# Delta-rule recurrence: bias carried by a weight row, v projected after the middle, late decays on VectorE, GpSimd's list reordered

## What is computed

```python
q = silu(causal_conv4(x @ Wq.T) + qcb)      # k (times 1/8) and v likewise, with kcb and vcb
a, beta = sigmoid(x @ Wa.T + ba), sigmoid(x @ Wb.T + bb)
def step(S, t):                              # S: 64 x 64 for each batch and head
    err = S @ k[t] - v[t]
    S = a[t][:, None] * S - beta[t] * err[:, None] * k[t][None, :]
    return S, S @ q[t]
o = layernorm(o, 64) * ln_w + ln_b           # then * sigmoid(x @ Wg.T), @ Wo.T, and x + that
```

## Time and profile before

| | |
|---|---|
| median of 3 runs | 4325.35 us (4315.23 to 4333.77) |
| the profiled execution | 4334.36 us, its span 4332.6 us |
| mean granted TensorE clock | 0.868 of full |
| TensorE, VectorE, ScalarE, GpSimd busy | 82%, 67%, 48%, 54% of the span |
| instructions | 127508 |

### The profile page before, as it was taken

How to read it: one execution, slowest core, us unless ns; L and a number is a source line. 1 busy time by engine, 2 the same in 40 slices (tenths; PEclk the granted TensorE clock), 3 DMA queues, 4 the chain that set the end, 5 groups by cost and what they waited for, 6 DMA issues and landing times. The chain is left out here.

```text
span 4332.6 us, 127508 instructions
## 1 busy us (share of the span) xinstructions
PE 3540.3 (82%) x53697; PEld 2464.3 (57%) x53697; DVE 2885.8 (67%) x6344; ACT 2090.6 (48%) x4778; POOL 2320.5 (54%) x3045
## 2 busy tenths in 40 slices
PE   6777888788787888878778777466999989988998
PEld 4555565555565556555555545354566647765765
DVE  4666666766667666666666766423788878865885
ACT  4243334343344333333333433233788869945992
POOL 1656566665666666676566666443101028815870
PEclk9788788887888888888788988668999989998999
DMA  3101110110111111011010101140000001101110
GB/s 83 33 27 36 29 35 26 39 35 25 36 29 35 33 32 35 25 39 36 24 34 26 34 28 30 34 131 28 2 2 2 2 21 37 41 15 30 38 41 25
DMA packets 156313, 140.11 MB, mean 32 GB/s; under 512 B 65350, under 2 KB 108578, under 8 KB 155486
## 3 DMA queue, kind: packets, MB, share of 16 engines
q1 hardware_dynamic: 153438, 129.25, 10.9%
q0 software_dynamic: 2304, 2.71, 0.2%
HBM read 96.12 MB, written 16.82 MB: 26 GB/s over the span
## 5 line engine op out<-in xcount | busy, mean ns | idle before, releaser
L1227 DVE TENSOR_TENSOR a_tmp<-a_h,banks 128x128 f32<-128x128 f32 (+6 forms) x896 | 434.1, 484 | 271.1 <-POOL a_h L944 252.2
L1233 DVE TENSOR_REDUCE a_h<-a_tmp 128x64 f32<-128x128 f32 (+6 forms) x896 | 434.2, 485 | 17.5
L1253 DVE STREAM_TRANSPOSE a_cross<-banks 128x1024 f32<-128x1024 f32 x64 | 80.0, 1250 | 449.6 <-PE banks L649 449.6
L944 POOL TENSOR_TENSOR a_h<-a_h,a_a 128x128 f32<-128x128 f32 (+3 forms) x512 | 279.5, 546 | 125.2 <-DVE a_h L1233 120.1
L763 ACT ACTIVATE a_va<-banks 128x512 f32<-128x512 f32 x128 | 136.8, 1069 | 407.5 <-PE banks L550 407.5
L928 POOL TENSOR_TENSOR a_st<-a_st,a_ab 128x512 f32<-128x512 f32 x256 | 326.0, 1274 | 0.0
L550 PE MATMUL banks<-a_w_v,a_xseg 128*32 128x512 f32 x2048 | 307.9, 756 | 0.0
L1001 POOL TENSOR_TENSOR a_cross<-a_cross,a_dk 128x128 f32<-128x128 f32 x64 | 35.9, 561 | 486.8 <-DVE a_cross L1253 486.8
L2097 ACT ACTIVATE c_s<-c_s,c_low 128x384 f32<-128x384 f32 (+1 forms) x512 | 266.3, 579 | 19.1 <-DVE c_low L2041 13.7
L833 ACT ACTIVATE a_st<-banks 128x512 f32<-128x512 f32 x128 | 69.5, 595 | 422.6 <-PE banks L679 422.6
L679 PEld LDWEIGHTS banks<-a_wt,a_kt 32*64 32x64 f32 x8192 | 158.8, 172 | 193.3 <-DVE a_wt L1270 193.3
(11 more groups left out here) (313 smaller groups left out, 9397.9 us busy)
## 6 DMA issues: line engine op xcount, KB each, us to landing
a_ab<-decays SPq DMA_DIRECT2D x512, 128.0 KB, 2.9
d_Vs<-d_V SPq DMA_DIRECT2D x128, 128.0 KB, 2.3
sent<-k_nothing SPq DMA_DIRECT2D x40, 64.5 KB, 2.4
b_xe<-sent SPq DMA_DIRECT2D x8, 322.5 KB, 3.5
a_xseg<-xn SPq DMA_DIRECT2D x32, 70.0 KB, 2.5
xn<-a_xnT SPq DMA_DIRECT2D x8, 256.0 KB, 2.7
a_xrow<-in_L_attn_x SPq DMA_DIRECT2D x128, 16.0 KB, 1.8
x<-a_xrow SPq DMA_DIRECT2D x128, 16.0 KB, 1.7
```

Source lines behind the costliest of these rows:

```text
L944: e.tensor_tensor(self.history(ch, t + 1)[:, :, lo:t], self.history(ch, t)[:, :, lo:t], at, ALU.mult).then_inc(*self.s_hist.at((g, t)))
L1227: e.tensor_tensor(prod, both, gram, ALU.mult).then_inc(*step.at((g, t, "product")))
L1233: e.tensor_reduce(self.results(ch, t), prod, AX.X, ALU.add).then_inc(*step.at((g, t, "w")))
```

## The change

- Bias. Weights q, k, v, a and g lose their last channel's column: GpSimd subtracts it from all 128 channels (the normed x sums to 0, so the last channel is minus the sum of the others). Partition 127 of `xn` becomes ones, written by DMA, and partition 127 of the turned weights gets the bias row by DMA (last tap). The bias matmuls (L545) are gone; q and k are emptied by one instruction with no bias instead of four.
- TensorE, second chunk: P, q half 1, two Gram products, moment dev, out, cross, v half 0, v half 1, carry, U. ScalarE follows: q, Gram products, out, root, cross Gram, v, v.
- VectorE decays the history of all steps 9 to 15; `act_gate_rows` copies their gates to PSUM. The reductions of the moments (`dve_moment`) and the transpose of the next Gram products (`dve_gram_rows`) move from between the steps to right behind the transpose L1249.
- GpSimd: `pool_history` only for steps 4 to 7, before `pool_second_half`; two of the four state decays come before the middle; `pool_first_half`, `pool_centre`, the other decays and `pool_query` behind it; `pool_scale` before `pool_prepare`. The second half's late right-hand side is one instruction instead of two.

```diff
@@ DeltaSetup.sync
-            e.dma_start(self.xn_dram[:, bi, PAD + t0:PAD + t0 + BANK], self.xnT[n % 2][:]).then_inc(*self.w_xn[n % 2].at(n))
+            e.dma_start(self.xn_dram[0:P - 1, bi, PAD + t0:PAD + t0 + BANK], self.xnT[n % 2][0:P - 1, :]).then_inc(*self.w_xn[n % 2].at(n))
+        for bi in range(NB):
+            e.dma_start(self.xn_dram[P - 1:P, bi, PAD:].rearrange("o (g x) -> o g x", x=P),
...
+        for n, bias, tap in (("q", "qcb", TAPS - 1), ("k", "kcb", TAPS - 1), ("v", "vcb", TAPS - 1), ("a", "ba", 0)):
+            q.wait_ge(self.s_wcopy, (n, 1, tap))
+            e.dma_start(a.wT[n][P - 1:P, tap, :], k["L0_attn_" + bias]).then_inc(*self.l_bias.at(n))
+        q.wait_ge(self.l_bias, "a")
+        q.wait_ge(self.w_ones, NB - 1)
@@ DeltaSetup.gpsimd
+        q.wait_ge(self.l_w, "all")
+        for n in PROJ:
+            e.tensor_copy(self.last[n][:], self.raw[n][:, :, D - 1:D]).then_inc(*self.s_last.at(n))
+            q.wait_ge(self.s_last, n)
+            e.tensor_tensor(self.raw[n][:], self.raw[n][:], self.last[n][:].broadcast_to([P, NCT, D]),
+                            ALU.subtract).then_inc(*self.s_less.at(n))
@@ DeltaRule.pe_project_rows
-        e.matmul(b, self.c.ones_row[0:1, 0:P], self.bias_row[n][:, part], start=True, stop=False)
@@ DeltaRule.tensor
             self.pe_P(e, q, s, 1)
-            if old >= 0:
-                self.pe_moment(e, q, old, "dev")
             if more:
                 self.pe_project(e, q, "q", nxt, 1)
                 for n in range(2):
                     self.pe_gram(e, q, nxt, n)
-                self.pe_project_rows(e, q, "v", nxt, 0)
-            self.pe_cross(e, q, s, 1)
+            if old >= 0:
+                self.pe_moment(e, q, old, "dev")
             if older >= 0:
                 self.pe_out(e, q, older)
+            self.pe_cross(e, q, s, 1)
             if more:
-                self.pe_project_rows(e, q, "v", nxt, 1)
+                for half in range(2):
+                    self.pe_project_rows(e, q, "v", nxt, half)
@@ DeltaRule.act_project
-        for m in range(4):
-            ct = 4 * half + m
-            src = b[:, m * SW:(m + 1) * SW].rearrange("p (b t) -> p b t", b=NB)
-            t = e.activation(self.kq[s % 2][:, ct * NB:(ct + 1) * NB, :, "kq".index(n)], src, ACT.Silu, bias=self.bias[n][:, ct:ct + 1])
-        t.then_inc(*self.s_evac.at((n, s, half)))
+        e.activation(self.kq[s % 2][:, half * R // 2:(half + 1) * R // 2, :, "kq".index(n)], b.rearrange("p (r t) -> p r t", t=SEG),
+                     ACT.Silu).then_inc(*self.s_evac.at((n, s, half)))
@@ DeltaRule.gpsimd, first chunk
             self.pool_rest(e, q, s, 0)
-            self.pool_history(e, q, s, 0, HAND, HAND + 1)
+            self.pool_history(e, q, s, 0, HAND, HC)
             self.pool_second_half(e, q, s, 0)
-            self.pool_history(e, q, s, 0, HAND + 1, HC)
-            if old >= 0:
-                self.pool_centre(e, q, old, 0)
+            for n in range(2):
+                self.pool_decay(e, q, g, n)
+            self.pool_cross(e, q, s, 0)
             self.pool_first_half(e, q, s, 0)
-            self.pool_cross(e, q, s, 0)
-            if old >= 0:
-                self.pool_centre(e, q, old, 1)
+            for n in range(2):
+                if old >= 0:
+                    self.pool_centre(e, q, old, n)
+            for n in range(2, 4):
+                self.pool_decay(e, q, g, n)
             self.pool_query(e, q, s, 0)
-            for n in range(4):
-                self.pool_history(e, q, s, 0, HC + HAND + n, HC + HAND + n + 1)
-                self.pool_decay(e, q, g, n)
@@ DeltaRule.dve_steps
-            if t < lo + HAND:
+            if t < HAND or lo:
                 at = self.abank[:, t, :].rearrange("p (i o) -> p i o", o=1).broadcast_to([P, 32, t - lo])
...
-            if t == HAND and s:
-                self.dve_moment(e, q, s - 1, "dev" if ch else "mean")
-            if ch == 1 and t == 10 and s:
+            if ch == 1 and t == 11 and s:
                 self.dve_reciprocal(e, q, s - 1)
-            if ch == 1 and t == 14 and s + 1 < self.nseg:
-                self.dve_gram_rows(e, q, s + 1)
@@ DeltaRule.dve_cross
         e.transpose(self.Wt[:].rearrange("p x i -> p i x"), self.W[ch]).then_inc(*self.s_wm.at(g))
+        if s:
+            self.dve_moment(e, q, s - 1, "dev" if ch else "mean")
+        if ch and s + 1 < self.nseg:
+            self.dve_gram_rows(e, q, s + 1)
         q.wait_ge(self.s_x, g)
```

More of the change, by code:

```diff
@@ L255, in __init__ @@
             self.tap = {n: sb("tap_" + n, [P, NCT, TAPS]) for n in CONV}
+            self.last = {n: sb("last_" + n, [P, NCT, 1]) for n in PROJ}
             self.raw_o = sb("raw_o", [P, CH])
@@ L549, in pe_project_rows @@
             for bi in range(NB):
[L550 removed]
+                t = e.matmul(b[bi * SEG:(bi + 1) * SEG, :], xs[:, bi, off:off + SEG], self.wT[n][:, j, part], start=(j == 0),
                              stop=(j == taps - 1))
@@ L900, in scalar @@
                     self.act_gram(e, q, nxt, n)
-                self.act_project_rows(e, q, "v", nxt, 0)
-                self.act_cross_gram(e, q, nxt)
             if older >= 0:
                 self.act_out(e, q, older)
+            if old >= 0:
+                self.act_root(e, q, old)
             if more:
-                self.act_project_rows(e, q, "v", nxt, 1)
+                self.act_cross_gram(e, q, nxt)
+                for half in range(2):
+                    self.act_project_rows(e, q, "v", nxt, half)
             self.act_state(e, q, g + 1)
@@ L1002, in pool_cross @@
         q.wait_ge(self.s_cross, (g, "mul"))
-        for odd in range(2):
-            e.tensor_tensor(self.history(ch, at + odd)[:, :, at + odd::2], self.P2[:, :, at + odd::2, 0], x[:, :, odd::2],
-                            ALU.add).then_inc(*self.s_rest.at((g, "late", odd)))
+        e.tensor_tensor(self.history(ch, at)[:, :, at:], self.P2[:, :, at:, 0], x, ALU.add).then_inc(*self.s_rest.at((g, "late")))
     def pool_query(self, e, q, s, ch):
@@ L1107, in gpsimd @@
             self.pool_rest(e, q, s, 1)
-            self.pool_history(e, q, s, 1, HAND, HAND + 1)
+            for t in range(HAND, HC):
+                self.pool_history(e, q, s, 1, t, t + 1)
+                if more and t > HAND:
+                    self.pool_cumulate(e, q, nxt, t - HAND - 1, t - HAND)
             self.pool_second_half(e, q, s, 1)
-            for t in range(HAND + 1, HC):
-                self.pool_history(e, q, s, 1, t, t + 1)
-                if more:
-                    self.pool_cumulate(e, q, nxt, t - HAND - 1, t - HAND)
-            if more:
-                self.pool_cumulate(e, q, nxt, 3, 5)
-            self.pool_first_half(e, q, s, 1)
-            self.pool_cross(e, q, s, 1)
-            if more:
-                self.pool_cumulate(e, q, nxt, 5, HC)
+            for n in range(2):
+                self.pool_decay(e, q, g, n)
+            self.pool_cross(e, q, s, 1)
+            self.pool_first_half(e, q, s, 1)
+            for n in range(2, 4):
+                self.pool_decay(e, q, g, n)
+            if more:
+                self.pool_cumulate(e, q, nxt, 3, HC)
             self.pool_query(e, q, s, 1)
-            for n in range(4):
-                self.pool_history(e, q, s, 1, HC + HAND + n, HC + HAND + n + 1)
-                self.pool_decay(e, q, g, n)
+            if old >= 0:
+                self.pool_scale(e, q, old)
             if more:
```

52 lines of the change are left out of this document (24 added, 28 removed).

## The result

| | before | after |
|---|---|---|
| median | 4329.56 us (4315.23 to 4337.09, 4 runs) | 3911.02 us (3909.59 to 3911.79, 4 runs) |
| ratio | | 0.9036 [0.9011, 0.9062] |
| the profiled execution, span | 4334.36, 4332.6 us | 3909.59, 3907.8 us |
| mean granted clock | 0.868 | 0.92 |

A forecast was written before the change was run, and what follows sets the result against it. VectorE's step-to-step chain, waiting for TensorE's cross product and GpSimd's decayed history, was the bound. Terms sum to -15.15 us per segment; thirty segments -454, edges -14, giving 3857 us; own range 3800 to 3950, 8-in-10 range 3790 to 4000.

The forecast's parts named there:

- a): VectorE's waits for GpSimd before step 6 and in steps 12 to 15 go: -7.9 us per segment.
- b): Middle, VectorE's wait for the cross product: 14.4 us per segment falls to 2.5 plus 2.7 in the two chunks, -9.2.
- rival of 13%: TensorE's clock stays low over v: v and carry end late, middle longer, +6 us per segment, 4040 us; chance 13%.
- c): Moment reductions and the Gram transpose move into the wait for the cross product and hide there: -1.55 us per segment.
- d): Decays of steps 9 to 15 on VectorE lengthen its chain: +2.0 us per segment, between 0 and +2.8.
- e): First chunk: U waits for centring, square, table load, k out, q half 0, carry: +1.9 us per segment, 0 to +3.
- f): First chunk's tail: GpSimd's gates no longer hold the state's add at L1279: -0.4 us per segment, 0 to -1.
- rival of a longer switch: Each ScalarE table switch costs a drain beyond its row, 1.4 us more per segment: 3898 us; chance 7%.
- g): ScalarE's merged q and k, wider gate copy, v behind the middle, later decay DMAs: all hidden, nothing on the path.
- h): Setup: subtractions 0 to +3 us, small DMAs 0 to +1, lost bias matmuls -2 to -4; taken as 0.

The follow-up runs named there:

- zero-row experiment: Changed kernel with each half of a and v again starting with a row matmul, of a zero row so values stay: 4010.04 us, ratio 0.9292.
- last experiment: Changed kernel with 128-row writes, plus both first-chunk centrings first in GpSimd's work behind the middle transpose, all four state decays behind it: 3823.18 us, ratio 0.8849.

## Why the prediction held, and where it failed

- **a) GpSimd's waits.** Right: none is left. The first halves fell by 3.16, where the waits (3.06) and the moved reductions (0.4) make 3.46. Alone in the kernel before the reordering gave 13 us of the 3.06 x 30 = 92 that its waits held, since there the middle was bound by TensorE.
- **b) The middle.** Right in size and place: -9.03 for -9.2, and in the second chunk v is the cause, with 209 us for it alone. The waits that are left, 2.32 us in the first chunk and 1.06 in the second, are close to the 2.5 and 2.7 reckoned, less the reductions and the transpose that now stand inside them. What the prediction did not have is the clock. It read the first chunk's wait in one segment (2.62 us, to become 2.5), while the mean there was 3.89; the sum took the mean over all chunks, and with it the difference. Its balance, lost bias matmuls against a VectorE that comes sooner, is right where the clock is full (4.49 before, 4.43 after); the mean fell by 1.41 us since the clock no longer falls there. The zero-row experiment shows what keeps it up: with the four row matmuls back it falls in 17 of 27 segments, as many as in the kernel before. The second chunk's middle is at 4.16 us in the mean where the clock is full, and at 7.1 to 8.3 in the 6 of 27 segments where it fell. In the one looked at (1293.3 to 1301.6 us) the granted clock was 0.70 and the dev moment took 3.78 us instead of 2.05. The low level over v was a rival of 13%; the low level came now and then, and before the cross product.
- **c) The Gram transpose.** Right in kind: 26 us measured for 1.16 x 30 = 35. The transpose on the second half costs 1.01 us, and the middle without it is 0.26 shorter, so it was not wholly hidden there.
- **d) Decays on VectorE.** Right: the second halves fell by 4.11 where a), c) and d) make 4.04. In the kernel before they fell by 3.12, where a) and d) make 2.88.
- **e) The new wait for U.** Right in place and cause, 14.33 us after the transpose's start for 14.7; the tail grew by 0.92. With f) the prediction had +1.5. U was 1.5 us behind VectorE (1418.39, 1416.86) for the 1.9 predicted. The last experiment removes it by starting the chain sooner. The rival of a longer switch falls. ScalarE in the same segment:

```profile
1409.62 1.06 ACT L852 ACTIVATE a_o<-a_o 128x1024 f32<-128x1024 f32 x1 [6.95 <-POOL a_o L1042]
1410.70 1.28 ACT L766 ACT_TABLE_LOAD   x1
1411.99 1.15 ACT L766 ACTIVATE a_kq<-banks 128x512 f32<-128x512 f32 x2
```

  The load starts 0.02 us after the square ends, and k 0.01 us after the load, with no drain between them.
- **f) L1279.** Right in kind: in the segment shown it takes 1.11 us (L1287 after) instead of 2.61. Its share of the tail was not measured apart.
- **g) Hidden work.** Right for v: v and the carry end 4.06 us before U.
- **h) The setup: the failed step.** "I take 0", with at most +3 for the subtractions and +1 for the small DMAs, stands against +46.4. The step priced the eight small DMAs, the subtractions and the lost matmuls, but not the eight large writes, whose only change is from 128 to 127 rows. They are the ones that pace the setup: 11.06 us each. Some 42 of the 46 went with 128 rows; the rest, 2.6 to 4, is within the step's bounds and was not taken apart. The forecast was 3857 and the kernel took 3911. This time lies inside the stated range because the range was wide for other reasons, a rival on the clock above all: no term and no rival held the step that missed.

The price was in the trace of before. A later layer there writes rows 1 to 127 of a tile (254 KB) beside one of 256 KB, and behind the burst of the latter the DMA engines stay at a share of 0.08, little more than one engine of sixteen, for 12 us and more. The window, with the DMA share and GB/s as its last two columns:

```profile
3655.00:3667.00 12.00, 11.82 (x148) 8.72 (x146) 10.38 (x17) 11.75 (x37) 10.54 (x9) 1.00 0.08 17
```

254 KB at 17 GB/s are 15 us. These bytes go in packets of 256, those of `xn` in packets of 2048, at the 24 GB/s of the window above. By the row of before the eight writes would have been priced at some 120 us of transfer, one behind the other (they took 88, 11.06 each), and the setup's end at tens of us instead of 0.

The pieces do not add up, and that was not seen in the sum either. Alone in the kernel before, v gives 209, the decays 71, GpSimd's order 13: 293 of 465. Taken alone from the changed kernel, v is worth 78, the row matmuls 99, the Gram transpose 26: 203. GpSimd's order shows why: it shortens a stretch that then waits longer for TensorE. The prediction's sum held because it asked of each stretch what is late next, with all edits in; the same terms used one at a time would have been wrong. That the clock went from 0.84 to 0.94 was in no term. It carries about 1.4 of the 15.3 us per segment in the first chunk's middle, which the prediction's mean of the waits took in unseen. How much it carries in the second chunk's, where no middle before ran at the full clock, was not measured alone. That the term of the middle comes within 0.2 us with no clock in it is in part luck.

## What to carry to other kernels

Give every DMA whose shape a change touches its own line in the sum: a slice shortened by one partition is not "a little less", and 127 rows took over four times as long as 128 here (11.06 and 13.7 us against 2.7). Here it paid to write all 128 and overwrite the one (3869 us instead of 3911). Cost edits of a loop across several engines stretch by stretch with all of them in, and look at what is late next: the same edit was worth 209 us in one surrounding and 78 in the other.

## What the runs showed of the hardware

- A write of 127 rows of 2 KB lands 13.7 us after its issue, one of 126 after 2.9, 125 after 4.0, 124 after 5.3, 120 after 2.4; one of 128 rows took 2.7 in the kernel before.
- Small VectorE instructions were held until a GpSimd instruction beside them ended. In the setup of the changed kernel (the VectorE rows have 24 elements per partition; in the kernel before each of them takes 0.18 us):

```profile
28.88 0.18 DVE L113 TENSOR_SCALAR a_rstd<-a_var 128x24 int32<-128x24 int32 x1
29.09 1.86 DVE L115 TENSOR_SCALAR a_rstd<-a_rstd 128x24 int32<-128x24 int32 x1
30.99 0.18 DVE L118 TENSOR_TENSOR a_part<-a_rstd 128x24 f32<-128x24 f32 x1
```
```profile
29.02 1.89 POOL L438 TENSOR_TENSOR a_raw_k<-a_raw_k,a_last_k 128x1024 f32<-128x1024 f32 x1
```

  Four of them took 1.86 to 1.87 us and one 0.76, each beside one of GpSimd's five subtractions. The 7.3 us that this adds moved VectorE's first weight scaling from 30.59 to 37.86 us. The Trainium skill, page "SBUF — State Buffer", section "Who interferes with whom", tells of a port pair that one of the two holds for a whole instruction; the rows fit that. Most of those 7 us are not on the path: with 128 rows the recurrence starts only 2.6 us later than before.
- 2.1 us of matmuls of one row, added to a full list, cost 3.6 us in the mean, since TensorE fell to its lower level around the cross product in 17 of 27 segments.
